# Three maximum banks, half-tile score banks and a split moved to the vector engine in an attention kernel

## The reference

```python
x = _layernorm(x + self_attention(x))
x = _layernorm(x + cross_attention(x, ctx))    # 16 heads of 8, 1500 keys, all in float32
x = _layernorm(x + ffn(x))                     # 128 -> 512 -> 512 -> 512 -> 128

# cross attention, per batch of 56 queries
scores = jnp.einsum('bhtd,bhsd->bhts', q, k) + bias      # bias depends on s - t alone
weights = jax.nn.softmax(scores, axis=-1)
attn = jnp.einsum('bhts,bhsd->bhtd', weights, v)
```

## Time and profile before

| | us |
|---|---|
| median of 3 runs | 1092.9 (1088.0 to 1096.4) |
| profiled execution | 1093.1 |
| its span, first to last instruction | 1091.3 |
| mean granted clock of TensorE | 0.952 |

### The profile page before, as it was taken

How to read it: one execution, slowest core, us unless ns; L and a number is a source line. 1 busy time by engine, 2 the same in 40 slices (tenths; PEclk the granted TensorE clock), 3 DMA queues, 4 the chain that set the end, 5 groups by cost and what they waited for, 6 DMA issues and landing times. The chain is left out here.

```text
span 1091.3 us, 25611 instructions
## 1 busy us (share of the span) xinstructions
PE 969.3 (89%) x10410; PEld 657.2 (60%) x10410; DVE 721.8 (66%) x1510; ACT 605.5 (55%) x1071; POOL 421.6 (39%) x418
## 2 busy tenths in 40 slices
PE   6754579999999999999999999989999988799996
PEld 3542256666666666666666666666666666545564
DVE  6565447878778877878778878876777774540014
ACT  2321157666667666666666666666666656352232
POOL 7330535554444555554444555554444400000000
PEclk9866689999999999999999999998999999899999
DMA  7507665555666655555665755554665420300000
GB/s 228 192 10 163 117 190 178 164 177 178 191 177 204 185 176 179 163 178 178 191 194 161 209 179 177 164 179 147 188 181 162 137 78 2 109 1 1 1 9 25
DMA packets 57388, 156.10 MB, mean 143 GB/s; under 512 B 23936, under 2 KB 36152, under 8 KB 54200
## 3 DMA queue, kind: packets, MB, share of 16 engines
q1 hardware_dynamic: 56744, 152.85, 48.1%
q10 hardware_dynamic: 528, 1.63, 0.4%
HBM read 111.63 MB, written 42.63 MB: 141 GB/s over the span
## 5 line engine op out<-in xcount | busy, mean ns | idle before, releaser
L769 ACT ACTIVATE e_sb<-st_ps 128x896 f32<-128x896 f32 (+1 forms) x384 | 354.1, 925 | 153.0 <-DVE st_ps L714 93.5
L108 DVE TENSOR_REDUCE cmax<-max_ps 112x1 f32<-112x512 f32 x512 | 337.6, 683 | 150.5 <-PE max_ps L98 150.4
L98 PE MATMUL max_ps<-kst,qst 111*112 111x512 bf16 x760 | 283.8, 401 | 37.8 <-PEq L117 14.1
L611 PEld LDWEIGHTS st_ps<-qst,kst 114*128 114x128 bf16 (+1 forms) x3072 | 191.7, 101 | 88.7 <-issue 41.8
L821 POOL TENSOR_TENSOR kpart<-k_left,kpart 128x500 bf16<-128x500 f32 x90 | 102.7, 1141 | 352.4 <-ACT k_left L787 347.8
L611 PE MATMUL st_ps<-qst,kst 114*128 114x112 bf16 (+1 forms) x3072 | 215.7, 213 | 19.5 <-DMA qst<-nmp 18.3
L105 DVE CUSTOM_DVE_ANT_0 near_out<-max_ps,near_nat 112x476 bf16<-112x476 f32 x248 | 154.0, 649 | 26.4 <-PE max_ps L98 26.4
L98 PEld LDWEIGHTS max_ps<-kst,qst 111*112 111x112 bf16 x760 | 92.2, 130 | 106.8 <-DVE cmax L108 38.9
L641 PE MATMUL pv_ps<-e_sb,vals 128*32 128x168 f32 (+1 forms) x3072 | 150.0, 313 | 0.3 <-ACT e_sb L769 0.3
L685 PEld LDWEIGHTS misc<-wv,ctxt 128*128 128x128 f32 (+1 forms) x768 | 99.6, 193 | 15.8 <-ACT vals L754 11.8
L641 PEld LDWEIGHTS pv_ps<-e_sb,vals 128*32 128x32 f32 (+1 forms) x3072 | 80.4, 109 | 47.1 <-issue 34.6
(11 more groups left out here) (127 smaller groups left out, 941.1 us busy)
## 6 DMA issues: line engine op xcount, KB each, us to landing
kst<-kparts SPq DMA_DIRECT2D x192, 375.0 KB, 6.2
kparts<-kpart SPq DMA_DIRECT2D x90, 375.0 KB, 2.7
ctxt<-in_ctxT SPq DMA_DIRECT2D x32, 750.0 KB, 7.4
qst<-qslots SPq DMA_DIRECT2D x192, 28.0 KB, 6.4
qslots<-qst SPq DMA_DIRECT2D x4, 672.0 KB, 11.2
kparts<-kst SPq DMA_DIRECT2D x6, 375.0 KB, 3.1
h<-in_h SPq DMA_DIRECT2D x2, 1024.0 KB, 8.6
qst<-nmp SPq DMA_DIRECT2D x96, 1.8 KB
```

Source lines behind the costliest of these rows:

```text
L98: return nc.tensor.matmul(dst[0:TT, 0:hi - lo], m.qst[0:M_ROW, r, p, :], m.kst[0:M_ROW, r, p, lo:hi], start=True, stop=True)
L108: return nc.vector.tensor_reduce(m.cmax[:, r, c, p:p + 1], src[0:TT, 0:BOUND[c + 1] - BOUND[c]], AX.X, ALU.max)
L611: mm = nc.tensor.matmul(st_ps[0:K, j % 2, p // 4, (p % 4) * TT:(p % 4 + 1) * TT], m.kst[0:AUG, u % RING, p, j * P:j * P + K], m.qst[0:AUG, ...
L769: nc.scalar.activation(e_sb[0:K, j % E_RING, :].rearrange("p (a c) -> p a c", a=2), st_ps[0:K, j % 2, :, 0:HALF], ACT.Exp).then_inc(s_ex, 1)
```

## The change

- `max_ps` has three banks in place of two; `st_ps` has three half tiles of one bank each in place of two tiles of two banks. Scores, near addition and exp of a tile are done in halves of four pairs, and the wait for a free score bank is made for each half: for the exp three halves back.
- The three parts of the maxima are made by DVE in step 7, right behind the reduction to `nmax`: copy to bfloat16, subtract, copy, subtract, each behind a semaphore of the one before. They lie in `nm3`, queries on the partitions.
- PE turns all three parts with one bfloat16 matmul in step 9 (`NMT`), behind the scores of that step and ahead of its first maximum chunk. ACT copies the result once, ahead of its exp of step 9, and SP writes it in one transfer.
- POOL has no more of this work, and multiplies by `own` before it splits key part 0.
- `x_own` and the sums behind it go from step 9 to step 7 (`XH`), `x_own` ahead of that step's chunks. In the first iteration the first values go from step 9 to 7.

```diff
-        max_ps = ctx.enter_context(nc.psum_tensor("max_ps", [P, 2, 512], F32))
-        st_ps = ctx.enter_context(nc.psum_tensor("st_ps", [P, 2, 2, 512], F32))
+        max_ps = ctx.enter_context(nc.psum_tensor("max_ps", [P, MAX_BANKS, 512], F32))   # 3
+        st_ps = ctx.enter_context(nc.psum_tensor("st_ps", [P, ST_BANKS, 512], F32))      # 3
...
-        HEAD_MISC = {4: ("k", 0, 3), 5: ("k", 1, 3), 6: ("k", 2, 3), M0: ("nmt", 0, 1),
-                     9: ("v", 0, 1), 10: ("v", 1, 1), 11: ("v", 2, 1)}
+        NMT = M0 + 1
+        HEAD_MISC = {4: ("k", 0, 3), 5: ("k", 1, 3), 6: ("k", 2, 3), NMT: ("nmt", 0, 1),
+                     7: ("v", 0, 1), 10: ("v", 1, 1), 11: ("v", 2, 1)}
...
-        NM, REC_A, REC_B, XH = M0 - 1, 4, 5, 9
+        NM, REC_A, REC_B, XH = M0 - 1, 4, 5, 7
...
# PE
-                wait(pe, s_ex, batch(g, u) * ST + j - 1)
                 K = st_rows(j)
-                for p in range(PAIRS):
+                for h in range(2):
+                    w = 2 * (batch(g, u) * ST + j) + h
+                    wait(pe, s_ex, w - ST_BANKS + 1)
+                    for p in range(4):
...
-                wait(pe, s_mr, batch(g, u + lag) * CHUNKS + n - 1)
-                max_scores(nc, m, max_ps[:, n % 2, :], r, c, p).then_inc(s_mx, 1)
+                wait(pe, s_mr, batch(g, u + lag) * CHUNKS + n - MAX_BANKS + 1)
+                max_scores(nc, m, max_ps[:, n % MAX_BANKS, :], r, c, p).then_inc(s_mx, 1)
...
                     if live(g, u):
                         scores(g, u, j)
+                    user = misc_user(g, u, j)
+                    if user and user[0] == "nmt":
+                        n = batch(g, u + user[2])
+                        misc_free(pe, g, u, j)
+                        pe.wait_ge(s_ib, 1)
+                        pe.wait_ge(s_nm, n + 1)
+                        nc.tensor.matmul(misc[0:3 * PAIRS, 0:TT], nm3[:, :, :].rearrange("q i p -> q (i p)"),
+                                         ident_b[:, :], start=True, stop=True).then_inc(s_nt, 1)
...
# DVE, step NM, behind the chunks of the step
                         nc.vector.tensor_reduce(nmax[:, :], m.cmax[:, (u + 1) % 2, :, :].rearrange("q c p -> q p c"),
-                                                AX.X, ALU.max, negate=True).then_inc(s_nm, 1)
+                                                AX.X, ALU.max, negate=True).then_inc(s_n0, 1)
+                        dve.wait_ge(s_n0, b + 2)
+                        nc.vector.tensor_copy(nm3[:, 0, :], nmax[:, :]).then_inc(s_n1, 1)
+                        dve.wait_ge(s_n1, 2 * b + 3)
+                        nc.vector.tensor_tensor(nm_left[:, :], nmax[:, :], nm3[:, 0, :], ALU.subtract).then_inc(s_n1, 1)
+                        dve.wait_ge(s_n1, 2 * b + 4)
+                        nc.vector.tensor_copy(nm3[:, 1, :], nm_left[:, :]).then_inc(s_n2, 1)
+                        dve.wait_ge(s_n2, b + 2)
+                        nc.vector.tensor_tensor(nm3[:, 2, :], nm_left[:, :], nm3[:, 1, :], ALU.subtract).then_inc(s_nm, 1)
...
# ACT
+                    if j == NMT and live(g, u + 1):
+                        act.wait_ge(s_nt, b + 2)
+                        if live(g, u):
+                            act.wait_ge(s_md[u % 2], filled(g, u, 2, 16))
+                        nc.scalar.copy(nmp[:, :], misc[0:3 * PAIRS, 0:TT]).then_inc(s_nr, 1)
...
+                        for h in range(2):
+                            w = 2 * (b * ST + j) + h
+                            if j < 2:
+                                act.wait_ge(s_nb, 4 * b + 2 * j + h + 1)
+                            act.wait_ge(s_st, w + 1)
+                            nc.scalar.activation(e_sb[0:K, j % E_RING, h * HALF:(h + 1) * HALF],
+                                                 st_ps[0:K, w % ST_BANKS, 0:HALF], ACT.Exp).then_inc(s_ex, 1)
...
-                            nc.scalar.copy(nmp[:, 0, :], misc[0:PAIRS, 0:TT])
-                            nc.scalar.copy(nm_left[:, :], misc[0:PAIRS, 0:TT]).then_inc(s_nr, 1)
...
# POOL
-                split_k(g, u, 0)
                 if live(g, u - 1):
                     pool.wait_ge(s_rc, 2 * b)
                     nc.gpsimd.tensor_tensor(rec[:, :].rearrange("p (i t) -> p i t", t=T),
...
                     pool.wait_ge(s_ro, b)
+                split_k(g, u, 0)
                 split_k(g, u, 1)
-                if live(g, u + 1):
-                    done = 3 * (b + 1)
-                    pool.wait_ge(s_nr, b + 2)
-                    nc.gpsimd.tensor_tensor(nmp[:, 1, :], nm_left[:, :], nmp[:, 0, :],
-                                            ALU.subtract).then_inc(s_np, 1)
...
# SP
-                    sp.wait_ge(s_np, 3 * (b + 2))
-                    for i in range(3):
-                        sp.dma_start(m.qst[M_ROW + i:M_ROW + i + 1, (u + 1) % RING, :, :],
-                                     nmp[:, i, :]).then_inc(s_md[(u + 1) % 2], 16)
+                    sp.wait_ge(s_nr, b + 2)
+                    sp.dma_start(m.qst[M_ROW:AUG, (u + 1) % RING, :, :],
+                                 nmp[:, :]).then_inc(s_md[(u + 1) % 2], 16)
```

More of the change, by code:

```diff
@@ L105, in reduce_scores @@
         return nc.vector.tensor_tensor_reduce(
-            out=m.near_out[:, p % 2, :], in0=src[0:TT, 0:FIRST_CH], in1=m.near_nat[:, p, :],
+            out=m.near_out[:, p % MAX_BANKS, :], in0=src[0:TT, 0:FIRST_CH], in1=m.near_nat[:, p, :],
             scale=1.0, scalar=LOWEST, op0=ALU.add, op1=ALU.max, accum_out=m.cmax[:, r, 0, p:p + 1])
@@ L606, in scores @@
                 if j == 0:
-                    pe.wait_ge(s_md[u % 2], filled(g, u, 2, 48))
-                wait(pe, s_ex, batch(g, u) * ST + j - 1)
+                    pe.wait_ge(s_md[u % 2], filled(g, u, 2, 16))
                 K = st_rows(j)
-                for p in range(PAIRS):
[L611 to L615, removed]
+                for h in range(2):
+                    w = 2 * (batch(g, u) * ST + j) + h
+                    wait(pe, s_ex, w - ST_BANKS + 1)
+                    for p in range(4):
+                        mm = nc.tensor.matmul(st_ps[0:K, w % ST_BANKS, p * TT:(p + 1) * TT],
+                                              m.kst[0:AUG, u % RING, 4 * h + p, j * P:j * P + K],
+                                              m.qst[0:AUG, u % RING, 4 * h + p, :],
+                                              start=True, stop=True)
+                    mm.then_inc(s_st, 1)
             def max_chunk(g, u, item):
@@ L668, in iteration @@
                         max_chunk(g, u, chunks[1])
-                    user = misc_user(g, u, j)
-                    if not user:
+                    if not user or user[0] == "nmt":
                         continue
@@ L705, in iteration @@
                     if j < 2 and live(g, u):
[L706 to L714, removed]
+                        for h in range(2):
+                            w = 2 * (b * ST + j) + h
+                            dve.wait_ge(s_st, w + 1)
+                            if j == 0:
+                                t, near = st_ps[:, w % ST_BANKS, 0:HALF], m.near_t0[:, h * HALF:(h + 1) * HALF]
+                            else:
+                                t = st_ps[0:NEAR - P, w % ST_BANKS, 0:HALF].rearrange("p (h t) -> p h t", t=T)
+                                t = t[:, :, T - NEAR + P:T]
+                                near = m.near_t1[:, h * HALF:(h + 1) * HALF].rearrange("p (h t) -> p h t", t=T)
+                                near = near[:, :, T - NEAR + P:T]
+                            nc.vector.tensor_tensor(t, t, near, ALU.add).then_inc(s_nb, 1)
                     if j == XH and live(g, u - 1):
@@ L868, in iteration @@
                 if later(g, u + 2):
-                    wait(sp, s_st, b * ST)
+                    wait(sp, s_st, 2 * b * ST)
                     if u + 2 == SA_K:
```

41 lines of the change are left out of this document (13 added, 28 removed).

## The result

| | before | after |
|---|---|---|
| median, us | 1092.0 (4 runs beside it) | 1178.9 (1174.6 to 1179.7, 4 runs) |
| ratio, 95% interval | | 1.079 (1.075 to 1.083) |
| span of the profiled execution, us | 1091.3 | 1172.8 |
| mean granted clock of TensorE | 0.952 | 0.907 |

The change makes the kernel 8% slower. The forecast was 1152, with a range of 1066 to 1200.

The account below looks back on a forecast made before the run. PE's in-order queue bounds the kernel, busy 23.37 of 24.51 us a batch. From 1093.1 us, +65.5 (29 batches at +2.26), -1.6 (last two batches) and -5 (late transfers) give 1152 us, range 1066 to 1200.

Parts of the forecast that it names:

- What bounds the kernel: Whole batch: the in-order PE queue sets the time, PE busy 23.37 of 24.51 us; gains must come from its idle time.
- The subtractions wait for POOL: Split on DVE: both SBUF subtractions wait for POOL's running instruction, ending at 485.2 and 486.4; PE stalls 2.4 us.
- POOL's phase: Beside the split: POOL's nine key instructions of 1.14 us, 0.08 apart, run without pause from near 480.3 to 491.2.
- The sum: Whole kernel: 29 batches at +2.26 us, last two gaining 0.8 each, late transfers -5; 1152 us from 1093.1.
- The rule cited from the Trainium skill: Split on DVE: two-port copies and casts also lock the port pair shared with POOL, so four instructions wait, not two.
- the rival built on it: Split on DVE: casts wait too, each for its own POOL instruction; stall 3.5 to 4.6 us, 1205 to 1235 us; chance 0.14.
- The way from the turn to the next batch: From PE's transpose in step nine to the next batch's first scores: PE needs only its own work, 4.4 us.
- The clock: PE after the stall: granted clock falls two times in three at 2.0 us, +1.35 us a batch (bounds 0 and 2.65).
- the late transfers: Two late maxima transfers before (waits 2.52, 1.64 us; 7.5 us with slow clock) fall mostly under 2 us slack: -5 us.
- The banks: Third maximum bank worth 0.15 us in steps zero to two; half tiles bring ACT to about 19 us, 0 on PE.
- The transfer: Single transfer of the maxima lands by 488.9, 2 us early, so PE's wait at the next batch's start goes.
- x_own at step seven: On DVE in step seven: waits 0.5 us for POOL, but DVE idles 0.96 us for PE there.

Follow-up runs that it names:

- e1: The changed kernel with POOL's key split cut from 500 to 20 columns of each part, so some computation is left out; 1062.9 us, 0.975 of the kernel before.
- e2: The changed kernel with the maxima and their remainder during the split kept in PSUM instead of SBUF, all work done; 1080.2 us, 0.990 of the kernel before.
- e8: The changed kernel with the split's two subtractions reading their first operand from PSUM, casts still SBUF to SBUF; 1123.0 us, 1.034 of the kernel before.
- e9: The changed kernel with the maxima's split in PSUM and POOL splitting the first third of keys before `own`; division in step seven; 1065.4 us, ratio 0.980.
- e7: The changed kernel with POOL splitting the first third of keys before `own` and the division back in step nine; 1153.2 us, 1.061 of the kernel before.
- e5: The changed kernel with eleven idle matmuls of 512 columns on PE ahead of its wait for the split; 1127.0 us, 1.033 of the kernel before.
- e10: The changed kernel with the old banks (two whole score tiles, two for maxima), split in SBUF; 1220.3 us, 1.123 of the kernel before.
- e12: As e9, but PE issues the turn of the split after the first maxima chunk of step nine; 1056.7 us, 0.972 of the kernel before.
- e6: The changed kernel with the split in PSUM, POOL splitting the first third of keys before `own`, and the division in step nine; 1071.6 us, ratio 0.988.
- e11: As e9, but with the old banks (two whole score tiles, two for maxima); 1102.5 us, 1.015 of the kernel before.

## Why the prediction was right, and where it was off

**What bounds the kernel.** Right: what moved the time moved PE's queue, by a wait or by the clock, and DVE's 2.9 us more of busy time in a batch cost only the waits for it.

**The subtractions wait for POOL.** Right, shown by e1 and e2: the sides of the wait can each be taken away. The forecast had them done 2.53 us behind the reduction's end (483.87 to 486.4); they were done 3.0 us behind it (552.12 to 555.12). The half microsecond is the first cast, which waited as well, and POOL's phase. I had set this phase by adding up POOL's instructions at 1.14 us, but the first lasted 1.84. The sum took both casts as free, and that was wrong: where the casts alone wait the gap is 1.80 us (e8), and 0.64 where nothing does (e9). The rule cited from the Trainium skill was right about the casts; the rival built on it, 3.5 to 4.6 us of stall, was not, because one cast did slip into a gap between two of POOL's. Which instructions slip through depends on POOL's phase (three waits in after, two in e7), and that it came out near two waits and a half microsecond is in part luck.

**The way from the turn to the next batch.** Forecast 4.4 us. In e9, at full clock, it is 622.78 - 618.43 = 4.35. Steps zero to nine became 0.65 us shorter (18.85 to 18.20), of which the forecast had 0.15 and put the rest into waits behind the turn. Together with the chain: +0.9 forecast, +1.5 at full clock (21.65 + 4.35 = 26.00 against 24.51; e5 has 25.92).

**The clock.** The mechanism was right; the frequency and the price were each off, in opposite directions. I took two falls in three at 2.0 us, +1.35. It falls in every steady batch, for 1.5 us (e5, e7, e8), so that 1.35 was near is partly luck. The price of 2.0 was the mean of 2.65 and 1.4 us. Both of those were the clock's, as the kernel before shows:

```profile
737.45:764.61 27.16, 26.06 (x300) 18.30 (x300) 19.15 (x39) 16.91 (x30) 11.74 (x13) 0.89 0.47 138
815.06:840.96 25.90, 24.80 (x300) 17.67 (x300) 19.10 (x39) 16.80 (x30) 11.74 (x13) 0.93 0.54 157
```

PE is busy 2.69 and 1.43 us longer there than in the earlier trace rows. The slow stretch was just longer the first time, and the stall in mid-batch brings the shorter one (0.94).

**The sum.** +59 us was forecast; the profiled spans differ by 81.5, the medians by 87. The term that was too small is the one for each batch, +0.9 +1.35, which measures +1.5 +1.5 = +3.0. On the spans the whole adds up: 28 steady batches at +3.0 are +84.0; the first batch took 28.63 us in place of 24.24, +4.4; the late transfers and small waits of the kernel before, gone after, are -8.3; two batches after of 28.84 and 28.88 us, in which the clock was low for longer (a mean of 0.88), make most of +2.1; and the last two batches gained 0.8 together, not each. That is +81.4. The -5 us for the late transfers was thus about right as a difference of -8.3 and +2.1, of which the second was not foreseen.

**The banks.** 0.15 us in the first steps was about right (0.10), and the exps in halves cost nothing on PE. ACT went to 17.1 us a batch, not to 19: the halves take 549 ns each, the 0.17 us more for each tile that I took, but they start 0.43 us apart, each beside the end of the one before, and one copy fell away. What I missed is that the new banks cover DVE's absence during the split, 1.2 to 1.3 us a batch at the same clock; without them the change would have cost 12% (e10).

**The transfer.** Right: its wait fell from 26.4 us to one of 6.3 at the start. **x_own at step seven** did not wait (0.44 us); POOL did.

## What to carry to other kernels

When a short chain moves from an idle engine to one on which others queue, count the wait of every instruction in it for the shared port, and then ask what is queued behind the chain and how many buffers cover that time. An operand in PSUM took a chain of 3.0 us down to 0.8 by a change of a few lines and, with the old order on POOL, turned a loss of 8% into a gain of 2%. An idle stretch of an in-order TensorE costs its length, and here often 1.5 us of clock on top: price both from batches at either level.

## What the runs showed of the hardware that I had not expected

DVE's `x_own` in step seven runs from 548.92 to 549.36, its 0.44 us alone, although POOL's key instruction had begun at 548.52; POOL's lasted 1.84 us in place of 1.14. The same pair is in all 28 steady batches of after and e2. POOL's instruction ends 0.99 to 1.01 us behind the end of `x_own` in every one, and 1.00 to 1.02 us behind it in e9 and e12, where it starts 0.05 us behind `x_own` and lasts 1.41 us. So it waits for `x_own` in both cases, whichever has the earlier recorded start. In e6, where the division meets a running POOL instruction in step nine, DVE waits (0.76 us):

```profile
625.56 0.76 DVE L725 TENSOR_TENSOR x_own<-x_sb,rec 128x280 f32<-128x280 f32 x1
```

In step seven `x_own` had been queued on DVE behind a reduction since before POOL's start. That it takes the port ahead of its own recorded start, or that POOL's recorded start is early, would explain the pair; no run here tests which. It matters because it moved POOL 0.7 us later.

The length of the gap alone does not decide the clock: with the same gap of 1.80 us e8 had batches at 1.00 and at 0.94, in no regular order, and one of e11's 28 steady batches, with the same stops of 0.32 and 0.69 us as the rest, had 0.94 and 26.67 us in place of 25.12.
